# Exponentials kept in PSUM over the logits, the softmax division moved to the outputs, and group statistics two batches ahead

## What is computed

```python
h = group_norm(x, gn_w, gn_b)              # 32 groups of 4 channels
q = einsum('bcn,oc->bno', hf, wq) + bq     # k, v alike
alpha = softmax(q @ k / sqrt(128))         # 1024 x 1024 for each batch
out = (alpha @ v) @ wo.T + bo + x
```

## Time and profile before

| | |
|---|---|
| median of 3 runs | 275.34 us (274.34 to 278.02) |
| the profiled execution | 273.92 us, its span 272.0 us |
| PE (TensorE matmul) busy | 215.7 us, 79% |
| DVE (VectorE) busy | 223.8 us, 82% |
| ACT (ScalarE) busy | 176.3 us, 65% |
| POOL (GpSimd) busy | 193.5 us, 71% |
| DMA queue of SyncE | 67.4% of 16 engines |
| mean granted TensorE clock | 0.925 of full |

### The profile page before, as it was taken

The page is one execution under the profiler, slowest core; times in us unless marked ns, Lnnn a source line. Parts: engine busy times, 40 slices in busy tenths (PEclk is TensorE's granted clock), DMA queues, the critical chain, the costliest instruction groups (busy, mean ns, idle before and its releaser), DMA issues.

```text
span 272.0 us, 3535 instructions
## 1 busy us (share of the span) xinstructions
PE 215.7 (79%) x1087; PEld 105.0 (39%) x1087; DVE 223.8 (82%) x419; ACT 176.3 (65%) x274; POOL 193.5 (71%) x181
## 2 busy tenths in 40 slices
PE   1993745999299966999489991999759996889984
PEld 1741322444144432544144441444325443434453
DVE  2769499899879988699869998799886998999841
ACT  2439384868576866467748585668674777888830
POOL 4055988499956996689966879559965899996040
PEclk9998697999889996899869996899968999999999
DMA  4203377567846687647974688566965876798893
GB/s 120 73 0 80 77 178 170 116 152 176 204 128 154 149 207 157 155 108 195 231 170 100 140 212 203 142 146 146 227 141 152 120 193 154 193 174 209 199 254 133
DMA packets 138323, 42.44 MB, mean 156 GB/s; under 512 B 134464, under 2 KB 135232, under 8 KB 138304
## 3 DMA queue, kind: packets, MB, share of 16 engines
q1 hardware_dynamic: 138016, 42.09, 67.4%
q10 hardware_dynamic: 288, 0.13, 0.2%
HBM read 4.46 MB, written 4.19 MB: 32 GB/s over the span
## 4 chain that ended last, share of the span: by engine, by line
PE 47%; DVE 26%; POOL 13%; issue 5%; ACT 4%; DMA 3%; SPq 0%; POOLq 0%; ACTq 0%; DVEq 0%
DVE neg_logits L699 10%; DVE parts L715 10%; PE S L407 7%; PE S L409 6%; PE S L411 6%; PE O L431 6%; PE O L432 6%; PE O L433 6%; DVE bn L645 3%; POOL u_lo L274 2%; POOL u_hi L271 2%; POOL h_lo L263 2%; PE M L337 2%; POOL h L257 2%; PE M L338 2%
## 5 line engine op out<-in xcount | busy, mean ns | idle before, releaser
L568 ACT ACTIVATE probs<-neg_logits,exp_bias 128x1024 f32<-128x1024 f32 x64 | 73.5, 1149 | 72.7 <-DVE neg_logits L699 72.6
L715 DVE SCALAR_TENSOR_TENSOR parts<-probs,row_inv,parts 128x1024 f16<-128x1024 f32 x64 | 105.5, 1649 | 1.1 <-ACT parts L579 1.1
L699 DVE TENSOR_SCALAR_CACHE_REDUCE neg_logits<-S,c_tok 128x1024 f32<-128x1024 f32 x64 | 81.6, 1275 | 27.7 <-PE S L411 23.9
L579 ACT ACTIVATE parts<-probs,row_inv 128x1024 f16<-128x1024 f32 x64 | 72.5, 1133 | 0.0
L407 PE MATMUL S<-h_hi,u_hi 128*128 128x512 f16 x128 | 41.4, 407 | 10.8 <-POOL u_lo L274 10.3
L433 PE MATMUL O<-pT,v_lo 128*128 128x512 f16 x120 | 48.0, 400 | 0.0
L432 PE MATMUL O<-pT,v_hi 128*128 128x512 f16 x120 | 48.0, 400 | 0.0
L431 PE MATMUL O<-pT,v_hi 128*128 128x512 f16 x120 | 47.8, 398 | 0.3 <-DMA pT<-parts 0.3
L409 PE MATMUL S<-h_lo,u_hi 128*128 128x512 f16 x128 | 40.8, 403 | 0.0
L411 PE MATMUL S<-h_hi,u_lo 128*128 128x512 f16 x128 | 40.0, 395 | 0.0
L304 POOL TENSOR_TENSOR y<-av,xres 128x512 f32<-128x512 f32 x15 | 19.6, 1309 | 27.2 <-ACT av L550 25.2
(11 more groups left out here) (108 smaller groups left out, 301.2 us busy)
## 6 DMA issues: line engine op xcount, KB each, us to landing
out_dram<-y SPq DMA_DIRECT2D x15, 256.0 KB, 2.7
x_sb<-in_x_dram SPq DMA_DIRECT2D x7, 512.0 KB, 4.5
pT<-parts SPq DMA_TRANSPOSE x64, 3.7
x_sb<-in_x_dram SPq DMA_DIRECT2D x2, 256.0 KB, 3.8
out_dram<-y SPq DMA_DIRECT2D x2, 128.0 KB, 1.9
wq_sb<-in_L_conv_wq_dram ACTq DMA_DIRECT2D x1, 64.0 KB, 3.2
wk_sb<-in_L_conv_wk_dram ACTq DMA_DIRECT2D x1, 64.0 KB, 3.7
wo_sb<-in_L_conv_wo_dram SPq DMA_DIRECT2D x1, 64.0 KB, 2.8
```

The costliest lines, as they stand in the source:

```text
L568: nc.scalar.activation(probs[:, T % PROBS, :], neg_logits[:, n % 2, :], ACT.Exp, scale=-1.0, bias=exp_bias[:, p, n:n + 1], accum_out=row_s ...
L579: nc.scalar.activation(parts[:, T % SPLITS, 0:N], probs[:, T % PROBS, :], ACT.Copy, scale=row_inv[:, p, n:n + 1]).then_inc(hi_done, 1)
L699: nc.vector.tensor_scalar(neg_logits[:, n % 2, :], S[n % 2][:, :], c_tok[:, p, n:n + 1], None, ALU.add, ALU.min, accum_out=exp_bias[:, p, ...
L715: nc.vector.scalar_tensor_tensor(out=parts[:, T % SPLITS, N:2 * N], in0=probs[:, T % PROBS, :], scalar=row_inv[:, p, n:n + 1], in1=parts[: ...
```

## The change

The number of PSUM tiles `S` becomes three, of `O` and `M` one each. The exponentials are written over the logits in `S[T % 3]`; both fp16 parts are made from there with the constant 4096 in place of the row's inverse, ScalarE's `high_part` right behind the exponentials of the same tile, `low_part` one tile later on VectorE, and `logits(T)` waits for `low_part(T - 3)`. Four tiles' inverses are taken by one reciprocal, written to DRAM, read back to all partitions (`write_inverse`, `spread_inverse` on SyncE's queue), and multiplied in by GpSimd before the residual is added, in two halves of VectorE at the very end. `x_sb` gets a third buffer, statistics are taken at n = 1 to 6 for batch b + 2, and the orders of all engines are rewritten. Blank lines are left out of the diff, and so are the waits by which `u`, `v`, mean and variance share the one tile `M`, the rest of the renamed semaphores, and `row_bias`, which is the `c_tok` instruction taken out of `v_parts`.

```diff
-    PROBS = 3
+    X = 3
...
-        scaled_sum = sb("scaled_sum", [128, 2, TILES], fp32)
-        row_inv = sb("row_inv", [128, 2, TILES], fp32)
-        probs = sb("probs", [128, PROBS, N], fp32)
+        row_inv = sb("row_inv", [128, 2, GT], fp32)
         parts = sb("parts", [128, SPLITS, 2 * N], fp16)
         pT = sb("pT", [128, 4, 2 * TILES, GT, 128], fp16)
+        inv_rows = sb("inv_rows", [C, 2, 128, GT], fp32)
         av = sb("av", [C, 2, GN], fp32)
+        attn = sb("attn", [C, 2, GN], fp32)
         y = sb("y", [C, 2, GN], fp32)
-        S = [pb(f"S{i}", [128, N], fp32) for i in range(2)]
-        O = [pb(f"O{i}", [C, GN], fp32) for i in range(2)]
-        M = [pb(f"M{i}", [128, HALF], fp32) for i in range(2)]
+        inv_line = nc.dram_tensor("inv_line", [2, 128, GT], fp32).ap()
+        S = [pb(f"S{i}", [128, N], fp32) for i in range(3)]
+        O = pb("O", [C, GN], fp32)
+        M = pb("M", [128, HALF], fp32)
...
+            def write_inverse(b, q):
+                eng.wait_ge(inv_done, 2 * b + q + 1)
+                if b >= 1:
+                    eng.wait_ge(rows_in[q], 16 * b)
+                eng.dma_start(inv_line[q, :, :], row_inv[:, q, :]).then_inc(line_out[q], 16)
+            def spread_inverse(b, q):
+                eng.wait_ge(line_out[q], 16 * b + 16)
+                if b >= 1:
+                    eng.wait_ge(attn_done, 2 * b + q - 1)
+                eng.dma_start(inv_rows[:, q, :, :].rearrange("c n t -> c (n t)"),
+                              inv_line[q, :, :].rearrange("n t -> (n t)").partition_broadcast(C)
+                              ).then_inc(rows_in[q], 16)
...
+            load_x(2)
             for b in range(B):
                 for n in range(TILES):
                     transpose(b, n)
-                    if n == 1 and b >= 2:
+                    if n == 0 and b >= 1:
+                        write_inverse(b - 1, 1)
+                    if n == 1 and b >= 1:
+                        spread_inverse(b - 1, 1)
+                    if n == 2 and b >= 2:
+                        store(b - 2, 0)
+                    if n == 4:
+                        write_inverse(b, 0)
+                    if n == 5:
+                        spread_inverse(b, 0)
+                    if n == 6 and b >= 2:
                         store(b - 2, 1)
-                    if n == 2 and b + 2 < B:
+                    if n == 6 and b + 3 < B:
                         eng.wait_ge(xres_done, b + 1)
-                        load_x(b + 2)
-                    if n == 5 and b >= 1:
-                        store(b - 1, 0)
+                        load_x(b + 3)
+            write_inverse(B - 1, 1)
+            spread_inverse(B - 1, 1)
+            store(B - 2, 0)
...
             def result(b, q):
-                eng.wait_ge(av_out, 2 * b + q + 1)
+                g = 2 * b + q
+                eng.wait_ge(rows_in[q], 16 * b + 16)
+                eng.wait_ge(av_out, g + 1)
+                nc.gpsimd.tensor_tensor(by_tile(attn[:, q, :]), by_tile(av[:, q, :]), inverses(q),
+                                        ALU.mult).then_inc(attn_done, 1)
                 eng.wait_ge(xres_done, b + 1)
+                eng.wait_ge(attn_done, g + 1)
                 if b >= 1:
                     eng.wait_ge(y_out[q], 16 * b)
-                nc.gpsimd.tensor_tensor(y[:, q, :], av[:, q, :], xres[:, b % 2, q * GN:(q + 1) * GN],
+                nc.gpsimd.tensor_tensor(y[:, q, :], attn[:, q, :], xres[:, b % 2, q * GN:(q + 1) * GN],
                                         ALU.add).then_inc(y_done, 1)
+            row_bias(0, 0)
             v_parts(0, 0)
             eng.wait_ge(ob_out, 1)
-            residual(0)
             for b in range(B):
+                if b >= 1 and b + 1 < B:
+                    h_parts(b + 1, 0)
+                if b == 0:
+                    row_bias(b, 1)
+                u_parts(b, 1)
+                if b >= 1:
+                    row_bias(b, 1)
+                if b == 0:
+                    h_parts(b + 1, 0)
+                if b + 1 < B:
+                    h_parts(b + 1, 1)
+                row_bias(b, 2)
                 v_parts(b, 1)
-                u_parts(b, 1)
+                v_parts(b, 2)
+                if b >= 2:
+                    result(b - 2, 1)
+                if b >= 2:
+                    eng.wait_ge(y_done, 2 * b - 2)
+                residual(b)
                 if b + 1 < B:
-                    h_parts(b + 1, 0)
+                    u_parts(b + 1, 0)
+                    row_bias(b + 1, 0)
+                    v_parts(b + 1, 0)
                 if b >= 1:
                     result(b - 1, 0)
-                if b + 1 < B:
-                    h_parts(b + 1, 1)
-                v_parts(b, 2)
-                if b + 1 < B:
-                    u_parts(b + 1, 0)
-                    v_parts(b + 1, 0)
-                if b >= 1:
-                    result(b - 1, 1)
-                if b + 1 < B:
-                    if b >= 1:
-                        eng.wait_ge(y_done, 2 * b)
-                    residual(b + 1)
+            result(B - 2, 1)
...
-                if T >= 2:
-                    pe.wait_ge(bias_done, T - 1)
-                s, q_hi, q_lo = S[n % 2], u_hi[:, p, n * 128:(n + 1) * 128], u_lo[:, p, n * 128:(n + 1) * 128]
+                if T >= 3:
+                    pe.wait_ge(lo_done, T - 2)
+                s, q_hi, q_lo = S[T % 3], u_hi[:, p, n * 128:(n + 1) * 128], u_lo[:, p, n * 128:(n + 1) * 128]
...
-                    if b >= 1:
-                        pe.wait_ge(av_out, 2 * b + q - 1)
+                    if b or q:
+                        pe.wait_ge(av_out, 2 * b + q)
+                    else:
+                        pe.wait_ge(v_out, NV)
...
-                    if n == TILES - 1 and b + 2 < B:
+                    if n == 0 and b == 0:
+                        group_mean(1)
+                    if n == 1 and b == 0:
+                        group_var(1)
+                    if n == 2 * (b == 0):
+                        project_u(b, 1)
+                    if n == 1:
+                        project_v(b, 1)
+                    if n == 2 + (b == 0):
+                        project_v(b, 2)
+                    if n == 4 and b + 2 < B:
                         group_mean(b + 2)
-                    if b == 0 and n == 0:
-                        pe.wait_ge(u_done, 1)
-                        group_mean(1)
-                    if n == (b == 0) and b + 1 < B:
-                        group_var(b + 1)
-                    if n == 0:
-                        project_v(b, 1)
-                    if n == 1 + (b == 0):
-                        project_u(b, 1)
-                    if n == 3:
-                        project_v(b, 2)
-                    if n == 5 and b + 1 < B:
+                    if n == 6 and b + 2 < B:
+                        group_var(b + 2)
+                    if n == 3 + 2 * (b == 0) and b + 1 < B:
                         project_u(b + 1, 0)
-                    if n == 6 and b + 1 < B:
+                    if n == 5 + 2 * (b == 0) and b + 1 < B:
                         project_v(b + 1, 0)
...
-                    act.wait_ge(y_done, 2 * b + q - 1)
-                nc.scalar.activation(av[:, q, :], O[q][:, :], ACT.Copy, scale=1.0 / P_SCALE).then_inc(av_out, 1)
+                    act.wait_ge(attn_done, 2 * b + q - 1)
+                nc.scalar.activation(av[:, q, :], O[:, :], ACT.Copy, scale=1.0 / P_SCALE).then_inc(av_out, 1)
...
                 act.wait_ge(bias_done, T + 1)
-                if T >= PROBS:
-                    act.wait_ge(lo_done, T - PROBS + 1)
-                nc.scalar.activation(probs[:, T % PROBS, :], neg_logits[:, n % 2, :], ACT.Exp, scale=-1.0,
+                nc.scalar.activation(S[T % 3][:, :], neg_logits[:, n % 2, :], ACT.Exp, scale=-1.0,
                                      bias=exp_bias[:, p, n:n + 1],
                                      accum_out=row_sum[:, p, n:n + 1]).then_inc(exp_done, 1)
             def high_part(b, n):
-                T, p = TILES * b + n, b % 2
-                act.wait_ge(inv_done, T + 1)
+                T = TILES * b + n
+                act.wait_ge(exp_done, T + 1)
                 if T >= SPLITS:
                     act.wait_ge(tr_in[(T - SPLITS) % TILES], 16 * ((T - SPLITS) // TILES + 1))
-                nc.scalar.activation(parts[:, T % SPLITS, 0:N], probs[:, T % PROBS, :], ACT.Copy,
-                                     scale=row_inv[:, p, n:n + 1]).then_inc(hi_done, 1)
+                nc.scalar.activation(parts[:, T % SPLITS, 0:N], S[T % 3][:, :], ACT.Copy,
+                                     scale=P_SCALE).then_inc(hi_done, 1)
...
+                    if n == 2 * (b == 0):
+                        copy_u(b, 1)
+                    if n == 1:
+                        copy_v(b, 1)
+                    if n == 2 + (b == 0):
+                        copy_v(b, 2)
+                    if n == 3 + 2 * (b == 0) and b + 1 < B:
```

(123 more changed lines are left out.)

88 lines of the change are left out of this document (49 added, 39 removed).

## The result

The changed kernel takes 263.33 us in the median of four runs (262.09 to 264.89), the kernel before 276.39 beside it: a ratio of 0.953 (0.944 to 0.963). The forecast was 243, from 234 to 262. The direction was right, more than half of the gain did not come, and the time lies just above the range.

The account below looks back on a forecast made before the run. TensorE's waits at the mean, their low clock, and VectorE-GpSimd blocking were taken as the losses. Setup 17.2, batch 0 26, six batches at 26.5, batch 7 19, tail 18.5 and 1.9 gave 241.6, forecast as 243 us, range 234 to 262.

Parts of the forecast that it names:

- hole at the mean: TensorE's wait for statistics at group_mean, 30.7 us in seven waits, with low clock behind each; claimed to vanish.
- Low part from PSUM: VectorE's low part with one PSUM input: 1.27 us instead of 1.65, saving 3.0 us a batch.
- no blocking: VectorE's low part no longer blocks GpSimd's SBUF reads; h_lo at 1.15 us throughout instead of 2.02 in the median.
- Inverses: VectorE drops two small instructions a tile for two reciprocals a batch: -2.5 + 0.3 us, busy time becoming 21.8.
- TensorE's floor: TensorE's work per batch at the high clock: 24.1 us, taken as a lower bound of a batch.
- SyncE's queue: Two added writes and two broadcasts a batch hide behind transposes; DMA time goes from 22.1 to about 24 us.
- the trip: Inverses written to DRAM and broadcast back, priced per batch as two more transfers like a store.
- the slack is nil: spread_inverse's wait for GpSimd's multiplication, with transposes queued behind: the inverses land at 21.9 us, wanted at 22.
- the walk: Engine-by-engine trace of one batch, giving 25 to 25.5 us with every slack just met; 26.5 was taken.
- The tail: Time behind the last row maximum: 18.5 us for 17.2, the second last store coming behind the last write and broadcast.
- Batch 7: The last batch's seven tiles at 2.6 us and a little each: 19 us for 20.85.
- slack missed: Rival, chance 0.20: some nil slacks cost 2.5 us a batch, short low clocks follow; batch 29, total 260 us.

Follow-up runs that it names:

- e11_before_x3: Kernel before with a third x buffer, loads at n = 0 and statistics of batch b+2 at n = 4: 262.51 us, ratio 0.948.
- e13_all_exp_sbuf: Changed kernel with padding, four inv_rows, fourth image buffer loaded at n = 1, early store, and exponentials in SBUF over three neg_logits: 281.94 us, ratio 1.017.
- e9_all: Changed kernel with 96 bytes of padding, four inv_rows, a fourth image buffer loaded at n = 1, and store(6, 0) early: 237.61 us, ratio 0.856.
- e2_before_shift: Kernel before with 32 unused bytes in front of parts, nothing else: 280.42 us, ratio 1.017.
- e1_align: Changed kernel with 96 unused bytes in front of parts, so parts and pT start at a multiple of 256 bytes: 254.97 us, ratio 0.921.
- e12_all_nopad: Changed kernel with four inv_rows, a fourth image buffer loaded at n = 1 and the early store, but no padding: 254.00 us, ratio 0.916.
- e10_align_no_trip: Changed kernel with 96 bytes of padding, without the inverses' writes, broadcasts and their waits (softmax division left out): 238.02 us, ratio 0.858.
- e7_inv4: Changed kernel with 96 bytes of padding and four inv_rows buffers, so spread_inverse waits for a multiplication two batches back: 244.92 us, ratio 0.875.

## Why the prediction was right, and where it failed

**The hole at the mean: right.** It went from 30.7 us to 5.5, and `e11_before_x3`, which takes it out of the kernel before, is 14 us faster.

**Low part from PSUM, and no blocking: right, and decisive.** The low part ran at 1.21 to 1.23 without spread, `h_lo` at 1.15 to 1.16. Against the 1.27 taken, it is 0.05 cheaper. The rule of fixed cycles in the Trainium skill (VectorE: DVE Perf Modes, The TRN2 errata), by which it would have cost, by an estimate, 0.06 more, is not borne out here. With both inputs back in SBUF, `e13_all_exp_sbuf` loses 44 us, by the longer low parts and GpSimd's longer instructions together. This agrees with the rule of the Trainium skill (SBUF — State Buffer, Who interferes with whom) that a VectorE instruction with two SBUF inputs and a GpSimd instruction that reads SBUF contend.

**Inverses and TensorE's floor: right.** VectorE was busy for 21.9 to 22.6 us in each of batches 1 to 5 of the changed kernel, against 21.8 forecast. Batches took 26.0, 26.0 and 24.8 there, and 24.4 to 24.7 in four of `e9_all`, against a floor of 24.1. The multiplication was 1.53 for 1.3: 0.46 a batch, on an engine with 33% idle.

**SyncE's queue: the step that failed.** The prediction said that writes and broadcasts "are taken behind transposes and hide", with DMA at "about 24" a batch. They do not hide: without them the changed kernel takes 241.14 us for 263.33. Two things were wrong in the step.

First, the price of a transpose was carried over from the earlier trace rows as if it could not change. It rose by 30%, 2.0 to 2.6 us, for an address that the diff never mentions; in `e2_before_shift` that alone is 29 us of the queue's time. `e1_align` gives 8.4 us of time for it, `e12_all_nopad` 16.4.

Second, the trip was priced as the DMA time of two stores, and what stands behind it in the queue was charged nothing. In the padded kernel it costs 17 us (`e1_align` against `e10_align_no_trip`), in the unpadded one 22. The DMA time of q1 does not settle how much of this is bytes. It rose by 33 us in the first pair (189.2, 0.805 x 235.0, to 222.0, 0.887 x 250.3) and by 17.5 in the second (219.6, 0.918 x 239.2, to 237.1), where I had 15 (8 x 1.9); packet times hold some waiting in a crowded queue. What is shown is the hold: of the 17, `e7_inv4` gets 10 back by loosening one wait, with every byte still moved. The prediction had looked at that wait, found that "the slack is nil", and sought its victim in the transposes behind it. Those were late (ScalarE waited 7.8 us for them), but the larger victim was the image load, an issue that the walk did not place on the queue at all: VectorE waited 19.5 us for it. The statistics at n = 1 need it, and the prediction tested that time only against TensorE's mean.

**The tail: failed by the same step.** 18.5 forecast, 28.1 measured. It named the second last store behind the last broadcast, and the chain shows this. But from the end of the last low part to the last broadcast it had 4.1 us (a transpose issue of 1.6, the write 2.5), where 10.1 went by: the chain has an earlier broadcast, two transposes of 3.04 and 2.62, and a store in between. The store took 4.30 for 2.7, and the last low part itself came 1.8 us late, its high part waiting for a transpose to land. In `e10_align_no_trip` the tail is 17.2.

**Batch 7: partly another slip.** It took 22.2 us for 19. But it takes 20.4 in `e10_align_no_trip` and in `e9_all` too, so 1.4 of the 3.2 us come from a term taken too low, seven tiles "at 2.6 and a little", and not from the queue. The total of `e10_align_no_trip` fits although this term was too low, because its batches 1 to 6, 25.5 us in the mean, came in under the 26 of its own sum: that much of the agreement is luck.

**The rival "slack missed"** gave 260 and was nearest. Its mechanism was half right: transposes held on SyncE, short low clocks. But it spread 2.5 us over each batch, whereas the loss comes in batches 3, 5 and 7 and the tail. It should have had a larger chance: by my own count ten waits had under 0.3 us to spare, and the sum held only if all ten did.

**Open.** Why one transpose of the changed kernel (tile 4 of batch 0) ran at the fast rate. Whether the address of `parts` or that of `pT` sets the price of a transpose: the padding always moved both. How the last 7.3 us by the medians (5.4 by the ratios) from `e7_inv4` to `e9_all` divide between the image buffer and the store. How the rest of the trip's cost divides between bytes and the order of the queue.

## What to carry to other kernels

Give every transfer that a change adds, and every one already there, a place in its queue's order, with who waits for it: a hold strikes whatever stands behind it, here an image load that nobody had looked at. When a diff adds, shrinks or drops any array, compare the start addresses and the packet times of the transposes, not only the lines that changed. A page in which no engine is full can still have a crowded DMA queue: multiply the queue's share by the span and add the new transfers to that sum before trusting that they hide. Take the sum as a warning and not as a floor, since kernels with shares of 90.1, 91.8 and 96.4% took 263, 241 and 238 us here.

## What the runs showed of the hardware

- A DMA transpose of 512 KB takes 2.0 us (about 290 GB/s) with source and destination at a multiple of 256 bytes in the partition, 2.6 us (about 215 GB/s) at 160 and at 32 bytes past one. The changed kernel and its padded version show it, and so do the kernel before and its shifted one; other offsets, and `parts` and `pT` apart, were not tried. In both kernels at the shifted address some stretches still ran at about 290 GB/s.
- A 256 KB broadcast out of 2 KB in DRAM landed in 4.1 us in the changed kernel, a 256 KB store in 2.7.
- ScalarE's exponentials of 1024 columns took 1117 ns into PSUM and 1149 ns into SBUF (the kernel before); the fp16 copy 1022 ns out of PSUM and 1054 out of SBUF (`e13_all_exp_sbuf`).
